# Middle taps of the keys moved one unit earlier in VectorE's program: an adaLN, conv-attention and expert-FFN kernel on one core

## What is computed

```python
y = cond_expert_mlp(x, cond_8)            # one of 8 experts per batch
Q, K, V = heads(y @ Wq.T + bq), heads(y @ Wk.T + bk), heads(y @ Wv.T + bv)  # 16 heads of 8
scores = einsum('bhqd,bhkd->bhqk', Q, K) / sqrt(8)
scores = conv1d_over_keys(scores, conv_w) + conv_b    # mixes the 16 heads, 3 taps along the keys
x = x + softmax(scores) @ V @ Wo.T + bo
x = x + top1_moe_ffn(lora_base(x, cond_8))            # 8 experts, capacity 128
```

## Time and profile before

| | |
|---|---|
| median of 3 runs | 234.47 us (234.33 to 234.51) |
| the profiled execution | 235.03 us, span of its instructions 233.2 us |
| TensorE busy | 220.3 us, 94% |
| VectorE busy | 192.0 us, 82% |
| ScalarE busy | 164.2 us, 70% |
| GpSimd busy | 165.9 us, 71% |
| middle taps (L572) | 31 instructions, 29.5 us, mean 951 ns, 744 to 1852 ns |
| maxima (L639) | 128 instructions, 91.5 us, mean 732 ns |

### The profile page before, as it was taken

One profiled execution on the slowest core, in us unless ns is written; L12 is line 12 of the kernel. 1 busy time (PEld: TensorE's weight loads), 2 busy tenths in 40 slices (PEclk: granted clock), 3 DMA queues, 4 the chain that ended last, 5 costly groups with the idle time before them and its releaser, 6 DMA issues.

```text
span 233.2 us, 5463 instructions
## 1 busy us (share of the span) xinstructions
PE 220.3 (94%) x1741; PEld 178.8 (77%) x1741; DVE 192.0 (82%) x484; ACT 164.2 (70%) x296; POOL 165.9 (71%) x193
## 2 busy tenths in 40 slices
PE   8999998789989998999999999999999999999990
PEld 8445785477868886888887887888788899989990
DVE  2469999989898988999799899979989777793460
ACT  2465598799689978989898978989898771205410
POOL 1019988699969996998989888898982803360775
PEclk9999999999999999999999999999999999999998
DMA  6994004536727563645645663555566350930233
GB/s 193 337 443 131 3 1 161 110 139 135 225 46 214 190 135 129 141 151 122 204 131 149 194 139 141 133 198 123 164 193 138 145 127 3 347 104 3 23 34 34
DMA packets 16117, 33.42 MB, mean 143 GB/s; under 512 B 1618, under 2 KB 12882, under 8 KB 15826
## 3 DMA queue, kind: packets, MB, share of 16 engines
q1 hardware_dynamic: 14514, 31.94, 46.0%
q0 software_dynamic: 1152, 0.52, 2.5%
q10 hardware_dynamic: 432, 0.71, 1.0%
HBM read 20.32 MB, written 13.37 MB: 144 GB/s over the span
## 4 chain that ended last, share of the span: by engine, by line
PE 80%; DVE 6%; DMA 5%; issue 3%; ACT 2%; SPq 1%; POOLq 1%; POOL 1%; DVEq 0%; ACTq 0%
PE tp L1107 13%; PE sc L955 12%; PE sc L957 11%; PE sc L956 10%; PE pvbank L975 6%; PE pvbank L973 5%; PE tp L1241 3%; PE sc L1219 3%; PE misc L1002 2%; DMA PT<-swap 2%; DMA swap<-w2s 2%; PE sc L1168 2%; PE sc L1171 2%; PE sc L896 2%; DVE Pb L639 1%
## 5 line engine op out<-in xcount | busy, mean ns | idle before, releaser
L424 ACT ACTIVATE Pb<-Pb,nbias 128x512 f32<-128x512 f32 x128 | 90.4, 719 | 22.4 <-DVE Pb L639 21.2
L639 DVE TENSOR_SCALAR_CACHE_REDUCE Pb<-sc,col 128x512 f32<-128x512 f32 x128 | 91.5, 732 | 10.9 <-PE sc L957 10.5
L955 PE MATMUL sc<-Kh,Ql 128*128 128x512 f32 x124 | 56.5, 456 | 1.8 <-POOL Kl L272 1.4
L1107 PE MATMUL tp<-cst,Pb 128*128 128x128 f32 x316 | 47.5, 273 | 2.7 <-ACT PT L469 2.2
L1107 PEld LDWEIGHTS tp<-cst,Pb 128*128 128x128 f32 x316 | 38.8, 140 | 14.7 <-ACT PT L469 4.7
L957 PE MATMUL sc<-Kh,Qh 128*128 128x512 f32 x124 | 48.9, 394 | 0.0
L956 PE MATMUL sc<-Kl,Qh 128*128 128x512 f32 x124 | 48.7, 393 | 0.0
L284 POOL TENSOR_TENSOR td<-ta,tc_ 128x512 f32<-128x512 f32 x31 | 43.7, 1409 | 2.6
L469 ACT ACTIVATE PT<-tp 128x512 f32<-128x512 f32 x77 | 44.8, 582 | 0.9 <-PE tp L1107 0.5
L272 POOL TENSOR_TENSOR Kl<-kc,Kh 128x512 fp32r<-128x512 f32 x28 | 36.1, 1291 | 12.9 <-ACT Kh L419 11.6
L778 DVE STREAM_TRANSPOSE w2s<-Pb 128x512 f32<-128x512 f32 x45 | 31.6, 703 | 0.0
(11 more groups left out here) (230 smaller groups left out, 298.7 us busy)
## 6 DMA issues: line engine op xcount, KB each, us to landing
swap<-w2s SPq DMA_DIRECT2D x15, 768.0 KB, 3.3
PT<-swap SPq DMA_DIRECT2D x60, 192.0 KB, 3.9
w1s<-in_w SPq DMA_DIRECT2D x1, 2048.0 KB, 10.3
w2s<-in_w SPq DMA_DIRECT2D x1, 2048.0 KB, 7.6
cst<-in_consts SPq DMA_DIRECT2D x1, 652.0 KB, 5.9
xTs<-in_xT SPq DMA_DIRECT2D x2, 256.0 KB, 3.6
we<-in_wexp SPq DMA_DIRECT2D x2, 256.0 KB, 4.0
b2s<-in_b2row SPq DMA_DIRECT2D x1, 512.0 KB, 11.1
```

The lines of the kernel that those rows point to most:

```text
L424: act.activation(Pb[:, k, :], Pb[:, k, :], ACT.Exp, bias=nbias[:, k:k + 1], scale=-1.0)\
L639: dve.tensor_scalar(Pb[:, k, :], SC[k % 4][:, :], cb, None, ALU.subtract, ALU.min, accum_out=nbias[:, k:k + 1]).then_inc(s["mx"], 1)
L955: pe.matmul(SC[k][:, :], ql, Kh[:, h2, :], start=True, stop=False)
L1107: mm = pe.transpose(bank[:, k * 128:(k + 1) * 128], Pb[:, u % RING, k * 128:(k + 1) * 128], ident)
```

## The change

The middle tap of a head stands one unit earlier, at the end of VectorE's units 1, 5, 9 and 13 instead of 2, 6, 10 and 14. Which head it serves and what it waits for are the same. The instructions of the other engines and their order are unchanged.

```diff
-                if u % QT == 2 and (not isinstance(g, int) or H * b + G * g + j + 3 < B * H):
+                if u % QT == 1 and (not isinstance(g, int) or H * b + G * g + j + 3 < B * H):
                     over = isinstance(g, int) and G * g + j + 3 >= H
                     middle_tap(H * b + G * g + j + 3, b + 1 if over else b,
                                G * g + j + 3 - (H if over else 0), (j + 1) % 2)
```

## The result

The changed kernel takes 233.52 us as the median of 10 runs (232.61 to 234.33), beside 234.81 for the kernel before on the same chip (10 runs, 234.33 to 235.70). The ratio is 0.9936, 95% interval 0.9917 to 0.9956: 1.5 us faster, by the interval 1.0 to 1.9. The forecast was 232.6, and 1.83 us of gain. The profiled execution took 232.92 us with a span of 231.09, against 235.03 and 233.20. Of those 2.11 us, 0.32 lie ahead of attention: the first tap starts at 22.50 instead of 22.82, with nothing changed there, so times of the two traces are compared less that 0.32; 1.79 are left for attention.

What follows compares the result with a forecast made beforehand. TensorE was taken as the bound from 60 to 190 us, stalled by late maxima behind taps waiting for GpSimd's sum. Gains 0.70 + 0.68 + 0.47 - 0.02 = 1.83 us: 234.47 - 1.83 = 232.64 us, range 231.9 to 234.1.

Steps and rivals of the forecast that it cites:

- What bounds the kernel: From 60 to 190 us almost all TensorE, losing about 0.8 and 1.1 us in groups 1 and 2 to late maxima.
- the turns: On the VectorE-GpSimd shared path, whoever asks first has it; a waiting tap ends 0.54 to 0.55 us after GpSimd's operation.
- Rival C: The tap's place doesn't matter: plain sharing, or the move is not on a path; 234.5 us, chance 0.09.
- Group 0, -0.47: Transposes of unit 15 come 0.47 us sooner, although the query operation and head 4's scores come later.
- Group 1, -0.68: Tap at unit 9 asks 0.11 us before GpSimd's sum and goes first, so the last maximum comes sooner: 0.68 us gained.
- Group 2, -0.70: Tap at unit 9 meets GpSimd's product instead of its sum, so the last maximum comes sooner: 0.70 us gained.
- Groups 3 to 7, +0.02: TensorE is the bound there, so the swap is nearly neutral: 0.02 us lost in all.
- The sum: All groups' terms together: 0.70 + 0.68 + 0.47 - 0.02 = 1.83 us gained.
- the race of group 1: Whether group 1's tap asks before GpSimd's sum is dispatched; forecast to win by 0.11 us.
- rival A: In group 1 the tap waits for GpSimd's sum, with two maxima behind: +0.67 there, 233.99 us, chance 0.15.
- B: Group 0's later query operation and low half are not made good: +0.5 for -0.47, 233.6 us, chance 0.12.
- D: GpSimd's sum has the path first in all three groups: 236.7 us; lighter form, groups 0 and 1, 235.3; chance 0.09 together.

Runs made afterwards that it cites:

- e3: Kernel before, taps at their old places, with GpSimd's sum td cut to 4 columns instead of 512: 232.57 us, ratio 0.9874.
- e4: Changed kernel, all taps one unit sooner, with GpSimd's sum td cut to 4 columns: 232.98 us, ratio 0.9912 against the kernel before.
- e9: Kernel before, taps at their old places, with GpSimd's sum td as two instructions of 256 columns: 232.74 us, ratio 0.9899.
- e5: Changed kernel, but the tap of head 4 in group 0 stays behind the query operation: 233.91 us, ratio 0.9927 against the kernel before.
- e6: The change in groups 0 to 2 only, old places from group 3 on: 233.95 us, ratio 0.9936 against the kernel before.
- e2: Kernel before with the taps of units 2, 6 and 14 one unit sooner, that of unit 10 kept: 234.00 us, ratio 0.9958.
- e7: Old places in groups 0 to 2, taps one unit sooner from group 3 on: 235.38 us, ratio 1.0004 against the kernel before.
- e8: The changed kernel run once more, nothing else changed: 233.78 us, ratio 0.9937 against the kernel before.
- e1: Kernel before with only the tap of unit 10 moved, to unit 9: 234.11 us, ratio 0.9955.
- e12: Changed kernel with the sum in two halves, head 4's tap in group 0 behind the query operation: 233.36 us, ratio 0.9909 against the kernel before.
- e10: Changed kernel, all taps one unit sooner, with GpSimd's sum td in two halves: 233.83 us, ratio 0.9947 against the kernel before.

## Why the prediction was right, and where its sizes were off

*What bounds the kernel, and the turns*: held. Each tap that meets a GpSimd operation ends 0.53 to 0.56 us after it, a halved sum shortens what is waited out to the half that is met, and a sum that is nearly gone takes the change's worth with it. Rival C falls with it as the cause in groups 0 and 2: e3 and e4 show what the place is worth where there is no sum to meet. (The prediction speaks of three taps over 1.1 us; the trace has six, of 1.11 to 1.85.) In group 1 the place did matter by itself, in a way that neither the working nor C has. The Trainium skill, GPSIMD Engine Reference, section 1 (Specifications), speaks of contention between the two engines; the traces agree (1.85 us for a tap that takes 0.75 alone), and e9 shows what that section leaves open, that it goes by whole instructions.

*Group 0, -0.47*: measured -0.45 (12.94 for 13.39), by the steps named, and handed on by the swap, which starts 0.46 sooner. Scores of head 4 expected near 42.5, read at 42.55; transposes of unit 15 near 46.8, read at 46.79; the query operation's delay was made good as worked out. e5 and e3 beside e4 show its price: 0.28 us of group 0 with the whole sum, 0.73 with a short one.

*Group 1, -0.68*: the step that failed. It measured -0.54, and not by a shorter turn. The forecast had the tap take 0.6 to 0.8 us instead of 1.18 and kept the 0.37 us of idle time ahead of unit 9's maximum. The tap took 1.15, and the idle time is gone, with 0.14 of smaller gaps: 0.51 of the 0.54. That the size comes near the forecast is luck. Why the tap met the second product, and not the gap ahead of the sum, can be followed. Without the idle time it starts 0.33 us sooner after the half-group's first scores. GpSimd comes 0.17 later: unit 6's maximum (57.76) now stands behind its tap, ScalarE's exponential waits 0.80 us for it, and the high half of the keys behind both comes at 60.26, 1.10 us after the first scores instead of 0.64; GpSimd's low half waits for that until 61.03. The working moved only VectorE's instruction and let GpSimd keep its place. The form that was forecast is e5's (0.75, and the sum 1.79), and with the idle time gone as well it gave 10.42. The other ending is e6's.

*Group 2, -0.70*: measured -0.89. The same shift, in the good direction: the tap came 0.13 sooner after its half-group's first scores (the idle time of 0.13 us ahead of unit 9's maximum is gone here too), GpSimd's second product 0.24 later (83.86 - 79.77 against 84.81 - 80.96), and the tap met the first product where I had it meet the second. That GpSimd's phase hangs on the taps before is what e2 showed by itself.

*Groups 3 to 7, +0.02*: -0.01 in the first trace, and e7 within its interval of nothing. The tap at 103.77 met a product, as said, and ended at 104.61.

*The sum*: 1.79 us of 1.83 in attention, by the first trace, and 1.50 by e8's. That the first is so near is in part luck: group 1 gave 0.14 less and group 2 0.19 more than forecast, and the first half-groups of groups 1 and 2 took 0.13 more, which the sum puts at nothing. The median gained 1.3 to 1.5; 233.52 lies 0.9 above 232.64, of which 0.34 are the kernel before (234.81 in 10 runs for 234.47 in 3). What the working lacked is the swap DMA of group 0's second half, which takes 4.2 to 5.3 us, so that TensorE waits 0.27 to 1.0 for it, and the race of group 1 can go with that. I gave this 0.15 as rival A and took it for a property of the kernel. That it is one of each execution, so that the median would lie between the two endings, fits e6 but isn't shown. B was right in kind for a faster group 0 (e1, e5): there it is the outputs before group 1 that take the gain. D did not come.

## What to carry to other kernels

Where two engines wait for each other's whole instructions on a shared path, the length of the longer instruction is a lever, and the place of the shorter one chooses what it meets: halving a sum of 1.29 us gave 2.4 us, moving the taps 1.5, and halving a low half that TensorE waits for as well took it all back. Compare the whole stretch between two fixed instructions and not only the one that you moved: half a microsecond of the gain was not in the tap. Before costing a moved instruction against the other engine's timeline, follow whether that engine's own start hangs on the moved one's followers. Where a race has 0.1 us of margin, the forecast should hold both endings: traces with the same instructions up to there (after and e6) went different ways.

## What the runs showed of the hardware that was not expected

- A turn costs the waiting side the rest of the other's instruction and 0.53 to 0.56 us for its own 0.67 to 0.75, in a sum, a half sum, a product and a low half alike.
- A swap DMA of 768 KB takes 3.25 to 3.29 us from its issue to that of the first transfer back in the 139 cases without a packet of instruction queue 8 beside it, and 3.42 to 5.65 in the 71 with one. The cause is not shown.
- VectorE is idle 0.37 us ahead of unit 9's maximum in group 1, and 0.13 in group 2, in the five kernels whose loop pass ends with that maximum, and not in the nine where a tap follows it. The cause is not shown.
- The granted clock fell to 0.50 for about 3 us after waits of 1.26 and 1.27 us in two executions, and not after 1.27 (after), 1.53 (e9) and 1.68 us (e12). From 40 to 42 us TensorE was busy 0.32 us in e12, less than the 0.74 in e10, and e12 kept the clock.
- With the same instructions up to group 2, second half-groups of group 1 of 10.58 (e8), 10.68 (after) and 11.36 us (e6).
